# A macaron block on one Trainium2 core: attention scores of two heads interleaved by 128 queries and made in 32-key column tiles, the narrow group as one exponential

## The reference: what is computed

```python
x = x + 0.5 * _L0_ffn_ref(_layernorm(x), w_gate, w_up, w_down)      # silu(x wg) * (x wu), then wd
x = x + _L0_attn_ref(_layernorm(x), norm_w, Wq, Wk, Wv, Wo, gate, log_temperature)
x = x + 0.5 * _L0_ffn_ref(_layernorm(x), w_gate, w_up, w_down)
```

```python
h = _rmsnorm(x, norm_w)
q = (h @ Wq)...; k = (h @ Wk)...; v = (h @ Wv)...      # heads of 32, k and v repeated twice
q = _l2norm(q); k = _l2norm(k)
attn = jnp.einsum('bhqd,bhkd->bhqk', q, k) * jnp.exp(log_temperature)
attn = jax.nn.softmax(jnp.where(causal, attn, -jnp.inf), axis=-1)
out = jnp.einsum('bhqk,bhkd->bhqd', attn, v)...
return x + gate * (out @ Wo)
```

## Time and profile before

| | |
|---|---|
| three timed runs | 447.05, 447.22, 448.2 us; median 447.22 |
| the profiled execution, its own time | 444.96 us |
| its span (first to last instruction) | 443.2 us |
| busy: PE, ACT, DVE, POOL | 93%, 84%, 81%, 58% of the span |
| granted TensorE clock | full (2.4 GHz) in all slices that were sampled |
| attention stage | 102 to 360 us of the span |

### The profile page before, as it was taken

One profiled execution on the slowest core, in us unless ns is written; L12 is line 12 of the kernel. 1 busy time (PEld: TensorE's weight loads), 2 busy tenths in 40 slices (PEclk: granted clock), 3 DMA queues, 4 the chain that ended last, 5 costly groups with the idle time before them and its releaser, 6 DMA issues.

```text
span 443.2 us, 10510 instructions
## 1 busy us (share of the span) xinstructions
PE 410.2 (93%) x3747; PEld 215.0 (49%) x3747; DVE 357.3 (81%) x943; ACT 372.7 (84%) x513; POOL 254.9 (58%) x325
## 2 busy tenths in 40 slices
PE   0689998989998999999999999999999999999995
PEld 0346565664434435435335335336345245676654
DVE  5989997799789788888887898898768948888654
ACT  4799999776886978978978978978968998999960
POOL 5689999984634534534535435432232458999851
PEclk9999999999999999999999999999999999999999
DMA  6486443516336054054072072082070114476452
GB/s 166 111 188 154 50 60 60 96 22 121 51 71 122 1 106 89 0 99 94 0 130 59 0 142 50 1 138 54 1 143 1 25 26 96 95 119 122 104 112 76
DMA packets 119215, 34.95 MB, mean 79 GB/s; under 512 B 101632, under 2 KB 119168, under 8 KB 119168
## 3 DMA queue, kind: packets, MB, share of 16 engines
q1 hardware_dynamic: 117888, 34.02, 39.9%
q10 hardware_dynamic: 1280, 0.33, 0.3%
HBM read 4.98 MB, written 4.19 MB: 21 GB/s over the span
## 4 chain that ended last, share of the span: by engine, by line
PE 27%; ACT 24%; DVE 22%; issue 15%; POOL 6%; DMA 5%; SPq 0%; DVEq 0%; ACTq 0%
ACT PT L829 8%; ACT XN L459 6%; PE ps L716 6%; PE ps L723 5%; PE ps L696 5%; PE ps L507 4%; DVE RD L241 4%; ACT SG L477 3%; DVE RT L1059 2%; DVE H L328 2%; ACT w_int L470 2%; POOL HL L434 2%; DVE SS L1044 2%; PE ps L749 2%; DVE QN L1098 2%
## 5 line engine op out<-in xcount | busy, mean ns | idle before, releaser
L829 ACT ACTIVATE PT<-ps,k_exp 128x1024 f32<-128x1024 f32 (+1 forms) x160 | 155.9, 1040 | 12.2 <-PE ps L702 9.6
L507 PE MATMUL ps<-XT,WT 128*128 128x512 f16 x384 | 94.8, 386 | 5.6 <-DVE H L328 1.8
L696 PE MATMUL ps<-QKT 128*128 128x512 f16 (+3 forms) x384 | 87.1, 328 | 5.8 <-ACT PT L829 4.2
L716 PE MATMUL ps<-PT,V 128*32 128x512 f32 (+3 forms) x768 | 78.5, 496 | 0.0
L723 PE MATMUL ps<-PT,ones 128*32 128x512 f32 (+3 forms) x768 | 76.6, 486 | 0.0
L434 POOL TENSOR_TENSOR HL<-H,HH 128x1024 f16<-128x1024 f32 x31 | 66.6, 2147 | 8.3 <-ACT HH L483 5.3
L328 DVE SCALAR_TENSOR_TENSOR H<-SG,k_isilu,ps 128x1536 f32<-128x1536 f32 x32 | 57.8, 1807 | 13.9 <-ACT SG L477 6.4
L507 PEld LDWEIGHTS ps<-XT,WT 128*128 128x128 f16 x384 | 34.6, 99 | 50.7 <-issue 10.0
L696 PEld LDWEIGHTS ps<-QKT 128*128 128x128 f16 x384 | 27.8, 97 | 56.0 <-ACT PT L829 49.0
L459 ACT ACTIVATE XN<-X,NB,RS 128x128 f32<-128x128 f32 x128 | 52.4, 482 | 2.7 <-POOL NB L406 2.6
L282 POOL TENSOR_TENSOR OL<-ON,OH 128x512 f16<-128x512 f32 x15 | 17.6, 1173 | 60.9 <-ACT OH L278 60.9
(11 more groups left out here) (139 smaller groups left out, 647.4 us busy)
## 6 DMA issues: line engine op xcount, KB each, us to landing
result<-X SPq DMA_DIRECT2D x15, 256.0 KB, 2.5
X<-in_L_attn_x SPq DMA_DIRECT2D x7, 512.0 KB, 4.3
X<-in_L_attn_x SPq DMA_DIRECT2D x2, 256.0 KB, 4.9
XT<-w_int SPq DMA_TRANSPOSE x32, 3.1
QKT<-ST SPq DMA_TRANSPOSE x18, 5.6
AXT<-AS SPq DMA_TRANSPOSE x16, 2.8
w_int<-in_L_ffn_w_gate SPq DMA_DIRECT2D x1, 192.0 KB, 4.2
w_int<-in_L_ffn_w_up SPq DMA_DIRECT2D x1, 192.0 KB, 4.6
```

The costliest lines, as they stand in the source:

```text
L507: i = e.matmul(out[:, j, :], WT[:, wp, w * NJ + j, :], XT[k % 2][:, xp, :], start=a == 0, stop=a == len(passes) - 1)
L696: i_ = e.matmul(SCORES[hp][:, h, o:o + n], QKT[k % 2][:, i // TPC, NH + hp, i % TPC * P:(i % TPC + 1) * P], QKT[k % 2][:, qc, 2 * hp + h, ...
L716: e.matmul(PVD[HD * h:HD * h + HD, 0, CH - n:CH], V[k % 2][:, i, v0:v0 + HD], PT[g % 2][:, h, o:o + n], start=i == 0, stop=i >= TPC * qc, ...
L829: e.activation(PT[g % 2][:, 2 * hp:2 * hp + 2, 0:n], SCORES[hp][:, :, 0:n], ACT.Exp, scale=k_exp[:, 0:1]).then_inc(a_exp, 1)
```

## The change

Scores of a pair of heads no longer lie head by head, but in alternate blocks of 128 queries (head 0, head 1, head 0, ...), and `pieces` cuts a tile's 2n columns at the bank boundary. Each piece, and each mask, is made by four matmuls, each with 32 keys as stationary operand (`COLUMN_TILES`), into one quarter of the partitions, all with the same moving queries. `slots` counts what a group needs of the two pairs of banks: two, or one for the narrow groups, whose two pairs of heads share one slot and one exponential. `PT` has the same layout as the scores, and `weigh` picks a head's blocks out of it (`weights_of`, `sums_of`). The counts of `a_s` and `a_exp` follow the slots (`NS` = 18 a batch instead of 20). On ACT, `stack_hi` of half 1 stands behind the exponentials of group 7 instead of 6, in batches from 1 on.

```diff
-        PT = [sb(f"PT{i}", [P, NH, CH]) for i in range(2)]
+        PT = [sb(f"PT{i}", [P, 2, 2 * CH]) for i in range(2)]
...
+        def slots(g):
+
+            return 2 if sum(n for _, _, n in groups[g][1]) == CH else 1
+
+        SLOT0 = [sum(slots(j) for j in range(g)) for g in range(NG)]
+        NS = sum(slots(g) for g in range(NG))
+
+        def score_bank(g, hp, col):
+
+            if slots(g) == 1:
+                return SCORES[SLOT0[g] % 2][:, hp, :]
+            return SCORES[(SLOT0[g] + hp) % 2][:, col // CH, :]
+
+        def pieces(o, n):
+
+            at = 2 * o
+            while at < 2 * (o + n):
+                end = min((at // CH + 1) * CH, 2 * (o + n))
+                yield at, end - at
+                at = end
+
+        COLUMN_TILES = [slice(c, c + HD) for c in range(0, P, HD)]
...
-                G = b * NG + g
-                if k * NG + g >= 1:
-                    e.wait_ge(a_exp, 2 * G + hp - 1)
+                single = slots(g) == 1
+                n_slot = SLOT0[g] + (0 if single else hp)
+                if k * NS + n_slot >= 2 and not (single and hp):
+                    e.wait_ge(a_exp, b * NS + n_slot - 1)
...
                 for i, o, n in tiles_:
-                    for h in range(2):
-                        i_ = e.matmul(SCORES[hp][:, h, o:o + n],
-                                      QKT[k % 2][:, i // TPC, NH + hp, i % TPC * P:(i % TPC + 1) * P],
-                                      QKT[k % 2][:, qc, 2 * hp + h, CH - n:CH], start=True, stop=True,
-                                      skip_group_check=o > 0)
-                    if i >= TPC * qc:
-                        for h in range(2):
-                            i_ = e.matmul(SCORES[hp][:, h, o:o + P], ident16[:, :], causal[:, :], start=False,
+                    masked = i >= TPC * qc
+                    rows = COLUMN_TILES
+                    key0 = i % TPC * P
+                    for at, w in pieces(o, n):
+                        q0 = CH - n + at // 2 - o
+                        q = QKT[k % 2][:, qc, 2 * hp:2 * hp + 2, q0:q0 + w // 2]
+                        dst = score_bank(g, hp, at)[:, at % CH:at % CH + w]
+                        for r in rows:
+                            i_ = e.matmul(dst[r, :].rearrange("p (s a n) -> p s a n", a=2, n=P),
+                                          QKT[k % 2][:, i // TPC, NH + hp, key0 + r.start:key0 + r.stop],
+                                          q.rearrange("p a (s n) -> p s a n", n=P), start=True, stop=True,
+                                          skip_group_check=o > 0)
+                    if masked:
+                        dst = score_bank(g, hp, 2 * o)[:, 2 * o % CH:2 * o % CH + 2 * P]
+                        for r in rows:
+                            i_ = e.matmul(dst[r, :].rearrange("p (a n) -> p a n", n=P), ident16[:, r],
+                                          causal[:, :].unsqueeze(1).to_broadcast([P, 2, P]), start=False,
                                           stop=True, skip_group_check=True)
...
+            def weights_of(g, h, o, n):
+
+                return PT[g % 2][:, h // 2, 2 * o:2 * (o + n)].rearrange("p (s a n) -> p s a n", a=2, n=P)[:, :, h % 2, :]
...
-                for hp in range(2):
-                    e.wait_ge(a_s, 2 * G + hp + 1)
-                    if hp == 0 and k * NG + g >= 2:
+                for i in range(slots(g)):
+                    e.wait_ge(a_s, b * NS + SLOT0[g] + i + 1)
+                    if i == 0 and k * NG + g >= 2:
                         e.wait_ge(a_pv, G - 1)
-                    e.activation(PT[g % 2][:, 2 * hp:2 * hp + 2, 0:n], SCORES[hp][:, :, 0:n], ACT.Exp,
+                    dst = PT[g % 2][:, i, :].rearrange("p (c n) -> p c n", c=2) if slots(g) == 2 else PT[g % 2][:, :, 0:CH]
+                    e.activation(dst, SCORES[(SLOT0[g] + i) % 2][:, :, :], ACT.Exp,
                                  scale=k_exp[:, 0:1]).then_inc(a_exp, 1)
...
-                        g_ = g - 1 if k == 0 else g
-                        if g_ in (4, 5):
-                            stack_hi(m0 + (g_ == 5), int(g_ == 5))
+                        g_ = 4 if k else 5
+                        if g in (g_, 6):
+                            stack_hi(m0 + (g == 6), int(g == 6))
```

More of the change, by code:

```diff
@@ L520, in gate_ @@
                 if ph and k == 0:
-                    e.wait_ge(a_exp, 2 * NG * B)
+                    e.wait_ge(a_exp, NS * B)
                 products(k, 0, G).then_inc(s_gate, 1)
@@ L673, in bank_uses @@
             return uses_in, await_full, await_read, seq, USE, home
-        def width(g):
-            return sum(n for _, _, n in groups[g][1])
+        def slots(g):
[13 more added lines that the diff above has]
+        COLUMN_TILES = [slice(c, c + HD) for c in range(0, P, HD)]
         def att_pe(e, shift, first=None, head=None):
@@ L704, in scores @@
-                i_.then_inc(a_s, 1)
+                    masked = i >= TPC * qc
[10 more added lines that the diff above has]
+                                          skip_group_check=o > 0)
@@ new lines, in scores @@
+                    if masked:
[3 more added lines that the diff above has]
+                                          causal[:, :].unsqueeze(1).to_broadcast([P, 2, P]), start=False,
+                                          stop=True, skip_group_check=True)
+                if hp or not single:
+                    i_.then_inc(a_s, 1)
@@ L706, in weigh, with sums_of @@
+            def weights_of(g, h, o, n):
+                return PT[g % 2][:, h // 2, 2 * o:2 * (o + n)].rearrange("p (s a n) -> p s a n", a=2, n=P)[:, :, h % 2, :]
+            def sums_of(h, i, n):
+                return PVD[HD * h:HD * h + HD, i, CH - n:CH].rearrange("p (s n) -> p s n", n=P)
             def weigh(k, b, g):
                 qc, tiles_ = groups[g]
-                G = b * NG + g
-                e.wait_ge(a_exp, 2 * G + 2)
+                e.wait_ge(a_exp, b * NS + SLOT0[g] + slots(g))
@@ L715, in weigh @@
                         v0 = DQ + DK + HD * (h // 2)
-                        e.matmul(PVD[HD * h:HD * h + HD, 0, CH - n:CH], V[k % 2][:, i, v0:v0 + HD],
-                                 PT[g % 2][:, h, o:o + n], start=i == 0, stop=i >= TPC * qc,
+                        e.matmul(sums_of(h, 0, n), V[k % 2][:, i, v0:v0 + HD],
+                                 weights_of(g, h, o, n), start=i == 0, stop=i >= TPC * qc,
                                  skip_group_check=True)
@@ L722, in weigh @@
                     for h in range(NH):
-                        i_ = e.matmul(PVD[HD * h:HD * h + HD, 1, CH - n:CH], ones32[:, :],
-                                      PT[g % 2][:, h, o:o + n], start=i == 0, stop=i >= TPC * qc,
+                        i_ = e.matmul(sums_of(h, 1, n), ones32[:, :],
+                                      weights_of(g, h, o, n), start=i == 0, stop=i >= TPC * qc,
                                       skip_group_check=True)
@@ L822, in exps @@
             def exps(k, b, g):
-                n = width(g)
                 G = b * NG + g
-                for hp in range(2):
-                    e.wait_ge(a_s, 2 * G + hp + 1)
-                    if hp == 0 and k * NG + g >= 2:
+                for i in range(slots(g)):
+                    e.wait_ge(a_s, b * NS + SLOT0[g] + i + 1)
+                    if i == 0 and k * NG + g >= 2:
                         e.wait_ge(a_pv, G - 1)
-                    e.activation(PT[g % 2][:, 2 * hp:2 * hp + 2, 0:n], SCORES[hp][:, :, 0:n], ACT.Exp,
+                    dst = PT[g % 2][:, i, :].rearrange("p (c n) -> p c n", c=2) if slots(g) == 2 else PT[g % 2][:, :, 0:CH]
+                    e.activation(dst, SCORES[(SLOT0[g] + i) % 2][:, :, :], ACT.Exp,
                                  scale=k_exp[:, 0:1]).then_inc(a_exp, 1)
@@ L1260, in qk @@
                 if m // QCS >= 2:
-                    e.wait_ge(a_exp, (m // QCS - 1) * 2 * NG)
+                    e.wait_ge(a_exp, (m // QCS - 1) * NS)
                 if m == 0 and not shift:
```

## The result

The changed kernel takes 460.63 us (median of 4 runs, 460.27 to 463.5); the kernel before, timed with it, 447.47 (4 runs). The ratio is 1.0307 with a 95% interval of 1.0263 to 1.035: 3.1% slower. The forecast was 451.3, slower, and its range ended at 455. The profiled execution took 460.76 us, with a span of 459.0 against 443.2.

A forecast was written before the change was run, and what follows sets the result against it. It took a per-batch loop of waits through PE, ACT and DVE as the bound. Batch 0 -0.2, batches 1 to 5 +6.3, batches 6 and 7 -2.0 gave +4.1 on 447.2: 451.3 us, range 440 to 455.

The forecast's parts named there:

- The moved step: ACT's stack_hi of half 1, batches 1 to 5: delays ST, AN and second AS; +1.25 us per batch, bounds +0.56 to +1.6.
- the walk: The prediction's trace of one batch's waits: ST 1.0 us later, eight AN taking 3.7, second AS 1.7 later.
- The terms that lead to ACT's group 7: PE's scores, weighing and masks (0.43, 1.72, 0.54), semaphore 0.04, drain 0.17 after 221.54: ACT starts group 7 at 224.49.
- Batches 6 and 7: The last batches, bound by PE and preparing no AN: fewer waits and shape changes were to save 2.0 us.
- The step that failed: Behind the wo projection in batches 1 to 5: PE idle about 2 us, counted within +1.25 us per batch.
- Sets in column tiles: PE's scores: four column tiles take 0.213 us per 512 columns, and twelve shape changes go, 1.3 us of PE per batch.
- rivals of dearer sets: PE's scores and masks: a set costs up to 0.43 us, giving some 60 us more, 507 us; chance 0.08.
- shape changes that still cost: Rival on PE: shape changes still cost 0.1 us each, so PE gains nothing; +5.9, 453.1 us; chance 0.08.
- PE's saving of 1.3 a batch: Twelve of 20 shape changes per batch go at 0.107 us each; little returns while the AN chain binds.
- more instructions are issued: Four PE matmuls replace one; issue was costed at nothing, from matmuls passing at 27 ns each.
- The faster rival: ST's move costs nothing because the AN end no later than now; 442.7 or 436.5 us; chance 0.22.
- Batch 0: First batch, keeping its ACT order and bound by the same AN: -0.2 us for PE's work ahead of it.

The follow-up runs named there:

- e4: The changed kernel with ten extra matmuls, results unused, behind the wo projection of batches 0 to 5 to keep PE busy; 452.23 us, ratio 1.0131.
- e1: The changed kernel without the moved step: stack_hi of half 1 back behind group 6, column tiles and single narrow exponential kept; 447.6 us, ratio 1.0025.
- e5: The changed kernel without the moved step and with PE's batches written out instead of a hardware loop; 443.87 us, ratio 0.9942.
- e10: The changed kernel without the moved step and without column tiles (128-key matmuls), leaving the narrow exponential and new column order; 445.94 us, ratio 0.9989.
- e7: The changed kernel with ACT's second AS of batches 0 to 5 put behind the next batch's first exponentials; 448.1 us, ratio 1.005.
- e9: The changed kernel without the moved step, PE's batches written out, and nine extra matmuls behind wo in batch 0; 442.88 us, ratio 0.9921.
- e2: The kernel before with only the moved step (stack_hi of half 1 behind group 7); 460.83 us, ratio 1.0324.
- e3: The changed kernel with scores in 128-column tiles again, moved step and narrow exponential kept; 461.25 us, ratio 1.0345.
- second set: The second of three groups of experiments, timed on one chip with its own runs of the kernel before, 445.9 us.
- e8: The changed kernel with the second AS one group later and PE's batches written out; 444.74 us, ratio 0.9959.

## Why the prediction was right in direction and wrong in size

**The moved step: right.** ST without a wait and 1.0 later (226.60 in before's frame), the AN meeting two POOL instructions (3.83 against 3.7), the second AS waiting 2.0 (over 1 forecast): each within 0.3 us. With the clock held (e4) a batch takes 34.21, which is +1.6, the upper bound that I gave, against the +1.25 I took. e4 as a whole is 5.9 us above before by its ratio, 6.5 by the medians of its set, against the +4.1 of the forecast; that its 452.23 looks so near to the forecast of 451.3 is in part luck, as before took 445.75 in that set and not 447.2. The 2 us between are 0.35 in each of five batches and 0.6 at the loop's jump. In the 0.35 lie the AS at 1.96 instead of 1.7 and the 0.9 us that wo waits for OL, which the walk did not have: it followed AN and AS, and OL only as what stands in their way. How the 0.35 divides between the two no run tells. (The terms that lead to ACT's group 7 add up to 224.44 and not to 224.49, which changes nothing.)

**Batches 6 and 7: right.** From the first reciprocal of batch 6 to the end of the span e4 takes 114.95 us, before 118.10. Of these 3.15 us 1.0 is only the later start of that reciprocal; 2.15 are left, against the 2.0 of the forecast.

**The step that failed** is "PE idle for about 2 us behind the wo projection, as today only behind batch 0 (1.72 ...)". The gap itself came (2.45, with 0.93 ahead of wo), but I priced it as a wait alone, "1.7 - 0.45 = +1.25 us per batch". The sum has no term for the clock, and so takes PE to resume at the rate at which it had stopped. In three of the six batches 0 to 5 it resumed at 1.2 GHz; in one it fell to that 0.1 us later, in two 1.5 and 1.7 us later. The one gap of this kind before the change, in the earlier trace rows, had the full clock behind it in that execution, but it is 1.72 long and no evidence for longer ones. The missing term is 7.9 us by the ratios (8.4 by medians): the forecast was +4.1, e4 with the clock held is +5.9, the changed kernel +13.7 (0.0307 x 447.5). Two of the six stretches are not the moved step's alone. Behind batch 0 the gap of 2.22 is that of e1 and e5 (2.23), which don't have the move, and between batches 2 and 3 the gap is 3.14, with the loop's jump in it. The Trainium skill, "TensorE: Matmul & The Clock Gate", section "HAM oscillation — how this bites in real kernels", describes a case of this kind, with longer waits (for DMA) that return with each turn of a loop and throttle the clock each time, and prices it at half of the throttled time. As an estimate by that page, the mean granted clock of 0.973 over 459.0 us makes 24.8 us at half rate and 12.4 of cost; the measurement gives 8. A part of the difference is seen in the traces. Some 3 us at half clock lie in the gaps themselves, where PE has nothing to lose, most of it ahead of 211.26 (PE busy 0.00, clock 0.50):
```profile
209.20:211.20 2.00, 0.00 (x0) 0.00 (x0) 2.00 (x5) 2.00 (x3) 1.19 (x1) 0.50 0.94 131
```
And a part of the slow matmuls lies where PE would have waited for ACT's second exponential anyway (0.17 in e4, no wait behind 247.36 in the changed kernel). The rest of the difference is not accounted for.

**Sets in column tiles: right.** Two sets and two masks between 238.65 and 239.30: 0.216 a set, 0.11 a mask, and no gap between them and the f32 sets on either side, where the earlier trace rows lost 0.12 and 0.10. The rivals of dearer sets and of shape changes that still cost are out. That PE's saving of 1.3 a batch buys little was right as well: e5 against e10 gives 0.3.

**Not in the sum:** the loop's jump, 3.7 us in e1 (36.0 against 32.3) together with the half clock behind it, 1.1 in e7 with full clock (34.25 against 33.17), and only 0.6 in the changed kernel with the clock held (34.80 against 34.21 in e4), where PE waits for ACT at that place anyway. I took "more instructions are issued" at nothing from the rate of issue; that was right for the rate and left out the length of the program.

**The faster rival** had as its condition that the second AS be less than 0.45 later; it is 1.96 later. **Batch 0** was to gain 0.2. With the clock held it gained nothing (33.57 in e9, 33.60 before), and in the changed kernel it lost its clock, although there the step doesn't move. Its gap behind wo was 1.72 before, 2.12 with the narrow exponential (e10) and 2.22 with the tiles: as it seems, what PE saves ahead of a wait that others set makes its idle time longer.

**What stays open** is when exactly the clock falls. Of the 14 gaps of 2.45 to 2.57 in the traces of the changed kernel, e2 and e3, 13 were followed by half rate, and the first one of e3 was not. Behind batch 0 gaps of 2.22 and 2.23 were (the changed kernel, e1, e5), gaps of 2.12 and 2.13 were not (e3, e10); one of 2.86 in e7 was not, those of 3.03 and 3.14 were (e1, the changed kernel). Behind those of 1.73 or less it did not fall in any trace. The length of the gap alone doesn't decide it.

Nor is it the same in each execution of one program. The 12 runs of e1 are four of 445.96 to 446.53 us with a mean clock of 0.993 or 0.994, and eight of 447.52 to 448.28 with 0.989 to 0.991. Of the 25 runs of before in the second set 13 take 444.72 to 445.90 with 0.998 or more, and nine take 446.76 to 447.29 with 0.993 to 0.996; so the kernel before seems to lose its clock at times too, but only an execution with the full clock was traced. In e4, e8 and e9 no run is under 0.998. The traces here show one execution each.

## What to carry to other kernels

Where an edit makes TensorE idle for more than 2 us once in each turn of a loop, price the stretch behind the gap at half rate as well as the gap; and before giving up such an edit, try cheap matmuls in the gap, for they tell the clock from the wait. A shift by 1 us of a step "with slack" is to be followed to each of its readers, OL as well as AN. Look at the clocks of all runs and not only at the trace, which is one execution. And where one instruction becomes four, look at the length of a hardware loop's body too: written out, the same tiles went from +0.25% to -0.6%.

## What the runs showed of the hardware

The granted clock fell to 1.2 GHz behind, or already in, PE's idle times of 2.2 to 3.1 us. It stayed full behind one of 2.46 (e3) and one of 2.86 (e7), and in every execution of e4 and e9, where matmuls whose results nobody reads fill the gap, the mean clock is 0.998 or more.

A DVE instruction on AN that starts while a POOL tensor_tensor runs stands still until that ends, and two POOL instructions back to back stop two in a row. One that has begun before is not stopped (e10: 342 ns at most). A reciprocal is not slower beside POOL's ST (3.34 at 237.83, where ST runs from 237.79 to 238.46). POOL of the changed kernel, and the eight AN by tile (duration in ns: shortest, median, longest):
```profile
242.64 1.29 POOL L282 TENSOR_TENSOR OL<-ON,OH 128x512 f16<-128x512 f32 x1 [4.18 <-ACT OH L278]
243.90 1.15 POOL L993 TENSOR_TENSOR AS<-AN,AS 128x512 f16<-128x512 f32 x1
```
```profile
L1063 DVE TENSOR_SCALAR AN<-X,AMV,RF x8: 331/340/1193, 241.8 to 245.3; 128x128 f32 x8
```
The eight take 2.14 with none stopped (e10), 2.99 with one, 3.83 with two.

Four f16 column tiles of 32 cost together what one of 128 columns costs: 0.216 us for 512 moving columns, and a mask of 256 columns in between 0.11.
